# Splitting the mixer's running maximum into three 16-bit parts: on VectorE or on GpSimd

## The chip, the cores and the metric

The kernel runs on one core of a Trainium2 chip. The metric is the device time of one execution in microseconds, as the median of several runs. Everything is one launch; the weights are prepared inside it.

## The reference

Two post-norm decoder layers over `x` of 16 batches x 256 tokens x 256 features, in float32, with a context of the same size:

```python
x = _layernorm(x + _L0_attn_ref(...))    # 16 heads, rotary positions
x = _layernorm(x + _L0_xattn_ref(x, ctx, ctx, ...))    # the mixer
x = _layernorm(x + _L0_ffn_ref(...))     # ternary weights, 8-bit activations
x = _layernorm(x + _L1_attn_ref(...))
x = _layernorm(x + _L1_xattn_ref(x, ctx, ctx, ...))
x = _layernorm(x + _L1_ffn_ref(...))
```

The change is in the second line, the mixer with 8 heads and exponential gates:

```python
csum = jnp.cumsum(jax.nn.log_sigmoid(ftilde), axis=-1)
Dtilde = where(lower triangle, csum[..., :, None] - csum[..., None, :], -inf) + itilde[..., None, :]
max_d = jnp.max(Dtilde, axis=-1, keepdims=True)
D = jnp.exp(Dtilde - max_d)
Ctilde = jnp.einsum('bhid,bhjd->bhij', qh, kh) * D / TAU
maxit = jnp.maximum(jnp.abs(jnp.sum(Ctilde, axis=-1, keepdims=True)), jnp.exp(-max_d))
Htilde = jnp.einsum('bhij,bhjd->bhid', Ctilde, vh) / (maxit + 1e-06)
```

With a = itilde - csum, the exponent is a[j] minus the running maximum of a up to i. So the matrix of decays needs only two rows of 256 numbers for each head.

## The kernel before, in words

A batch of 256 tokens is one unit of work. The 16 batches are dealt to four lanes, and each lane has its own set of tiles (`XO`, `YX`, `PB`, `QK`, `U`, `GN`, `M3` and others; the trace cuts the digit off, so `M3` reads `M`). A lane does its four batches one after the other; they are called rounds 0 to 3 here (`it` in the code). The lanes are interleaved, so that one lane's scores lie beside another's feed-forward layer.

Each batch goes through a list of some 130 steps (`lane_steps`). `PARTS` says which engines have a part in a step. What sets the order is `TURNS`: for every engine a string of digits, each digit a lane, that merges the lanes' lists into one fixed program for that engine. So each engine works through a written order and stops at a wait until it is met, whatever stands behind it. A step in which an engine is named but for which it has no code (for instance `v` of the first attention on VectorE) only takes a digit. `PLACES` gives the PSUM bank of each use.

The steps of the mixer that matter here, for one batch:

- `gates`: TensorE makes the gate inputs (L836). ScalarE makes the log-sigmoid (L1023 to L1029). VectorE, on 8 partitions x 256 elements, runs a sum scan (L1204), an add (L1206), a maximum scan into `G[7]` (L1208) and a subtraction (L1210), whose signal is `max_d`. Then it splits the running maximum into three bfloat16 parts, which go to partitions 0, 32 and 64 of `M3`: copy the high part (L1211), subtract it (L1213), round the rest (L1215), copy that (L1217), subtract it (L1218), copy what is left (L1220, signal `m_lo`).
- `vm`: TensorE centres the values, ScalarE copies them (L1033), GpSimd writes a column of ones (L1354).
- `turn`: TensorE transposes `GT` (L850) after `max_d`; VectorE copies `aT` (L1223); ScalarE makes `eneg` (L1039).
- `decay`, four times: TensorE multiplies a selection matrix with `M3` (L858, L860) and adds the mask (L859, L861); ScalarE takes the exponential (L1047, L1049). The first of the four waits for `m_lo`. Each has L858 twice.
- `mix`: TensorE makes the products of queries and keys (L872); VectorE multiplies them with the decays (L1229).
- `mixv`, `mixnorm`, `mixvar`, `mixscale`: values, transposition, normalization; VectorE's last operation, L1256, is `scaled`.
- `mixout`: GpSimd multiplies by a row and adds the stream (L1357, L1361), which frees the way to the next norm.

GpSimd has besides: `rope` (L1342, the rotary adds), `xb` (L1347, adds a row of biases to the stream of a lane), and the memsets of ones (L1351, L1354).

VectorE's other large work is the maximum of the scores in `max` (L1170, one reduction over 1024 PSUM elements for each pair of heads), for which TensorE makes the scores (L767).

`own` gives an instruction a signal on its engine's own semaphore and `wait_own` waits for it; with it an engine waits for its own earlier result:

```python
n = own(dve.tensor_tensor(Gl[:, 0, :], Gl[:, 7, :], M3[L][0:MH, :], ALU.subtract))
wait_own(n)
n = own(dve.tensor_copy(Mm[L], Gl[:, 0, :]))
wait_own(n)
dve.tensor_copy(M3[L][32:32 + MH, :], Mm[L]).then_inc(mix_dve[L], 1)
```

Of the kernel before, what the change touches and what calls it, by code (L numbers as in the profile page):

```python
# [12 lines left out]
ALU = mybir.AluOpType  # L13
# [11 lines left out]
MH, MHD = 8, 32  # L25
# [20 lines left out]
    "store": "sp", "gates": "pe act dve", "vm": "pe act pool", "turn": "pe dve act", "decay": "pe act",  # L46
# [98 lines left out]
def lane_program(lane):  # L145
# [7 lines left out]
    for at in range(-1, batches):  # L153
# [30 lines left out]
        "0012000311242211332000000000301003011011110110121010221000002010122201022122220311111120331022021233"  # L184
        "3003333122210233221300101321130123213311123333221033203002200300300200023230231203011330110310111113"
        "3131211312221222122122232222333332332320333300033310000003121113002320121221102212211022100200000120"
        "0200110123111133211133333332232313120103022233230000002203310030301111033013101110331110002300122122"
        "1012102221211220021311023333023033120332330031221202230101302112033211221333312311221033220030002000"
        "0002033000123110123203203111111131313111333132112222222220222022020300200203320330033033313303033310"
        "1130000130311111211001222022212220012102211112121112112232323313332333303220300023220000330200310311"  # L190
        "0130313011011303030011331310020122220122021201122221130211303202330112332003322203313013100322132322"
        "1303213331312313021212111030223000030000000023022302330132011113111131113111123212231222012222232000"
        "2220002000220001011113110333301130300003311333132313313300300122022212222021112112111231122333212333"
        "2223333320230000003220003020320033333003333310111011103111100110020122120221202122120232111103311203"
        "1202103213303320333122232101032120110323123320131323311222330220300020030023000032221303130110331011"
        "1111331133111320102122122222222322223333323332133231131333111113011131003000010002001202221220222022"
        "122311113303322333333330032232202310203333330"),
    "dve": (
        "0012210004321344311220000000044111111141223223202220033300330010031010033011020112112002210121201121"
        "3200013100232120100302302123013123321313132112313132010233000223232202223323111333131333130002022012"  # L200
        "0200112111113222332232223300330333120012200001033030001110000011113212213312112111222122030302203333"
        "2202231300331130011330333010120100212010221010321113003211220000321230002010222111332332113121113103"
        "1203030302223032222213232211133310000103330030333312211222112111022220303333222302003011100030320332"
        "1121330111300000011112212231223113211222200022033033222333001300133103033033113201002210022101201113"
        "0002131232102000233021332100202113321123321131111110312330002220330222322302021211001031000331332221"
        "1121231313231130322202022223313330031100000330333301112331020021110001012112121123112332220003332332"
        "2320223022330033130013130033101101200112210101212112020311223030122132300102023213000020213312312311"
        "3113131302203302023223222220331311133133013333001102122111211200200333223023222132213130330033332221"
        "33311222333000"),
    "pool": (  # L210
        "0022211033030032110112210320113332230000110302223111220330012231313102122003331122333010022000111102"
# [1188 lines left out]
```

## Time and profile before

| | |
|---|---|
| median of 3 runs | 1620.26 us |
| lowest and highest | 1614.66 and 1622.32 us |
| the profiled execution | 1622.2 us, its span 1620.4 us |
| mean granted TensorE clock | 0.969 |
| busy: TensorE, VectorE, ScalarE, GpSimd | 1465.2, 1183.2, 950.7, 225.4 us |
| instructions on GpSimd | 233 |

The profile is of one execution. A line such as L858 is a line of the kernel; a helper's line stands for all who call it. A timeline row gives the start and the duration in us, the engine, the line, the operation, what is written and read, how many instructions were merged into the row, and in brackets the idle time before it and who ended that. A granted clock of 1.00 is the full TensorE clock. Spans on GpSimd are rough.

### The profile page before, as it was taken

The numbers are of one execution on the slowest core, as the hardware profiler recorded it, in microseconds if no ns is written. First come the engines' busy times: TensorE is split into PE (matmuls) and PEld (weight loads), VectorE is DVE, ScalarE is ACT, GpSimd is POOL, SyncE is SP. The second block draws the span as 40 slices with busy tenths as digits, with TensorE's granted clock in tenths as the row PEclk, the third lists the DMA queues.
The fourth block names the chain that finished last, engine by engine and source line by source line (L and its number), as shares of the span: only waits on it lengthen the run. The fifth ranks groups of instructions, "written<-read, shape, count | busy, mean of one in ns | idle before, by whom it ended". The sixth has DMA issues, their size and how long they took to land. (4 is left out here: it accounts for less than half of the span.)

```text
span 1620.4 us, 31692 instructions
## 1 busy us (share of the span) xinstructions
PE 1465.2 (90%) x12482; PEld 972.9 (60%) x12482; DVE 1183.2 (73%) x2103; ACT 950.7 (59%) x1701; POOL 225.4 (14%) x233
## 2 busy tenths in 40 slices
PE   7588799899999879899999888998999988898998
PEld 4155556557766556557767555565776656465577
DVE  5978887865568888974765888866565788888632
ACT  3378466674466757566355666656545586655752
POOL 6011100002221011002212210000122111100100
PEclk9699989999999999999999898999999999999999
DMA  8430113322121021521321011331322101133200
GB/s 273 139 102 2 52 47 105 118 60 79 53 69 51 2 63 48 152 67 58 119 73 53 1 47 33 93 108 50 111 72 66 53 2 46 47 97 110 70 1 26
DMA packets 115074, 114.34 MB, mean 71 GB/s; under 512 B 9842, under 2 KB 100722, under 8 KB 114930
## 3 DMA queue, kind: packets, MB, share of 16 engines
q1 hardware_dynamic: 114610, 111.28, 22.4%
q8 instruction: 102, 1.67, 0.4%
q10 hardware_dynamic: 320, 1.05, 0.3%
q14 instruction: 42, 0.34, 0.1%
HBM read 68.91 MB, written 42.99 MB: 69 GB/s over the span
## 5 line engine op out<-in xcount | busy, mean ns | idle before, releaser
L1170 DVE TENSOR_REDUCE nm<-psum 128x4 f16<-128x1024 f32 x384 | 455.1, 1223 | 100.3 <-PE psum L767 99.2
L1005 ACT ACTIVATE PB<-psum 128x1024 f32<-128x1024 f32 x288 | 288.3, 1024 | 87.1 <-PE psum L786 85.7
L804 PE MATMUL psum<-PB,V 128*32 128x256 f32 x2304 | 206.8, 390 | 7.4 <-ACT PB L1005 5.2
L1347 POOL TENSOR_TENSOR XO<-XO,row_b 128x512 f32<-128x512 f32 x80 | 103.2, 1300 | 749.8 <-ACT YX L976 749.8
L767 PE MATMUL psum<-QK 48*128 48x256 f16 x1536 | 140.4, 280 | 46.8 <-DVE nm L1170 22.7
L786 PE MATMUL psum<-QK 49*128 49x256 f16 x1536 | 138.3, 277 | 21.4 <-ACT PB L1005 5.3
L767 PEld LDWEIGHTS psum<-QK 48*128 48x128 f16 x1536 | 58.9, 96 | 109.8 <-DVE nm L1170 38.8
L786 PEld LDWEIGHTS psum<-QK 49*128 49x128 f16 x1536 | 54.2, 95 | 111.4 <-issue 42.1
L930 PE MATMUL psum<-YX,W 128*128 128x256 f32 x512 | 120.0, 385 | 0.0
L804 PEld LDWEIGHTS psum<-PB,V 128*32 128x32 f32 x2304 | 79.9, 110 | 62.6 <-issue 20.0
L938 PE MATMUL psum<-W,PB 128*128 128x256 f32 x512 | 116.3, 382 | 0.0
L1005 ACT ACTIVATE YX<-psum 128x1024 f32<-128x1024 f32 x96 | 98.7, 1028 | 20.3 <-PE psum L786 20.0
L804 PE MATMUL psum<-YX,V 128*32 128x256 f32 x768 | 101.3, 385 | 5.1 <-ACT PB L1005 4.9
L930 PEld LDWEIGHTS psum<-YX,W 128*128 128x128 f32 x512 | 94.4, 190 | 17.3 <-issue 4.2
L938 PEld LDWEIGHTS psum<-W,PB 128*128 128x128 f32 x512 | 95.8, 190 | 13.9 <-issue 1.7
L694 PE MATMUL psum<-W_o,YX 128*128 128x256 f32 x384 | 97.8, 401 | 1.1 <-ACT YX L1012 0.5
L1111 DVE TENSOR_SCALAR XO<-YX,mv,rstd 128x256 f32<-128x256 f32 x192 | 79.5, 457 | 24.6 <-ACT rstd L960 24.3
L1009 ACT ACTIVATE U<-psum 128x512 f32<-128x512 f32 x112 | 66.9, 599 | 50.6 <-PE psum L804 43.3
L681 PE MATMUL psum<-cst,XO 128*128 128x128 f32 x512 | 81.8, 283 | 13.3 <-DMA XO<-in_x 4.2
L694 PEld LDWEIGHTS psum<-W_o,YX 128*128 128x128 f32 x384 | 73.1, 199 | 16.1 <-issue 2.6
L681 PEld LDWEIGHTS psum<-cst,XO 128*128 128x128 f32 x512 | 58.4, 142 | 38.9 <-issue 16.3
L1189 DVE TENSOR_TENSOR YX<-psum,XO 128x512 f32<-128x512 f32 x48 | 33.0, 688 | 64.3 <-PE psum L694 44.4
(171 smaller groups left out, 2675.4 us busy)
## 6 DMA issues: line engine op xcount, KB each, us to landing
QK<-heads_dram SPq DMA_DIRECT2D x96, 512.0 KB, 3.8
heads_dram<-U SPq DMA_DIRECT2D x288, 128.0 KB, 2.0
XO<-in_x SPq DMA_DIRECT2D x16, 256.0 KB, 3.2
YX<-in_ctx SPq DMA_DIRECT2D x16, 256.0 KB, 3.4
out<-XO SPq DMA_DIRECT2D x16, 256.0 KB, 2.5
W<-in_w SPq DMA_DIRECT2D x2, 1024.0 KB, 6.9
heads_dram<-PB ACTq DMA_DIRECT2D x4, 256.0 KB, 9.4
W_gu<-in_w_down SPq DMA_DIRECT2D x1, 1024.0 KB, 5.6
```

The costliest lines, as they stand in the source:

```text
L681: ins = pe.transpose(bank[:, k * TOK + t * P:k * TOK + t * P + P], src[:, t, k * P:(k + 1) * P], ident)
L694: ins = pe.matmul(bank[:, t * DIM:(t + 1) * DIM], xt(k)[:, t * P:(t + 1) * P], w[:, k], start=(k == 0), stop=(k == n - 1))
L767: ins = pe.matmul(b[:, e * 512 + t * TOK:e * 512 + (t + 1) * TOK], QS[L][r, unit, t * P:(t + 1) * P], KS[L][r, unit, :], start=True, stop= ...
L786: ins = pe.matmul(b[:, e * 512 + t * TOK:e * 512 + (t + 1) * TOK], KS[L][r, unit, t * P:(t + 1) * P], QS[L][r, unit, :], start=True, stop= ...
L804: ins = pe.matmul(b[SLOT * j:SLOT * j + SLOT, at:at + TOK], value(L, t, PAIRS * e + u, HEADS, HD, SLOT), src, start=(t == 0), stop=(t == T ...
L930: ins = pe.matmul(b[:, m * TOK:(m + 1) * TOK], W_1[:, k, c:c + P], XT_[L][:, k, :], start=(k == 0), stop=(k == KT - 1))
L938: ins = pe.matmul(b[:, 0:DIM], hid1(L, k)[:, unit * P:(unit + 1) * P], W_2[:, k], start=(k == 0), stop=(k == IT - 1))
L1005: act.activation(weights_of(L, unit), b[:, 0:1024], ACT.Exp, scale=HD ** -0.5)\
L1009: act.activation(flat2(U[L][:, unit - 1:unit + 1, :]), b[:, 0:512], ACT.Copy).then_inc(u_ready[L], 1)
L1111: dve.tensor_scalar(stream(L, it)[:, t], Y[L][:, t], mv[L][:, t, 0:1], rstd[L][:, t:t + 1], ALU.subtract, ALU.mult).then_inc(x_ready[L], 1)
L1170: dve.tensor_reduce(nm[L][:, :, :, unit].rearrange("p t e -> p e t"), b[:, 0:1024].rearrange("p (e t k) -> p e t k", e=2, t=TT), AX.X, ALU ...
L1347: pool.tensor_tensor(stream(L, it), stream(L, it), row_b[:, occ:occ + 1, :].to_broadcast([P, TT, DIM]), ALU.add).then_inc(xb_ready[L], 1)
```

## The change

The six operations go from VectorE's part of `gates` to a new part on GpSimd. They signal on a semaphore of their own, `max_parts`, three times for a batch, and TensorE's first `decay` waits for that. VectorE ends the step with `max_d`. GpSimd's order gets the 16 `gates` steps. The first lines are of the tables, the others of the code; of the digits only GpSimd's are shown.

```diff
-    "store": "sp", "gates": "pe act dve", "vm": "pe act pool", ...
+    "store": "sp", "gates": "pe act dve pool", "vm": "pe act pool", ...
...
     "pool": (
-        "0022211033030032110112210320113332230000110302223111220330012231313102122003331122333010022000111102"
-        "22300113330113322221003203311313022000211111122003232223330001112030023213133332233110122203"),
+        "0002221113330032100011122210320031113332223300010022311112220330233100131102212200033331112223330020"
+        "0011111022223013003330111322221000332331113330222000011111122023222333300001111220002321331133333222"
+        "31012203"),
...
-MIX_DVE = ("a", "max_d", "m_hi", "m_mid", "m_lo", "aT", "c0", "c1", "c2", "c3", "den", "last", "var", "scaled")
+MIX_DVE = ("a", "max_d", "aT", "c0", "c1", "c2", "c3", "den", "last", "var", "scaled")
...
+        max_parts = lane_sem("max_parts")
...
                     if unit == 0:
-                        pe.wait_ge(mix_dve[L], nth(MIX_DVE, it, "m_lo"))
+                        pe.wait_ge(max_parts[L], it * 3 + 3)
...
                     dve.tensor_tensor(GT[L][32:32 + MH, :], Gl[:, 7, :], Gl[:, 6, :], ALU.subtract).then_inc(mix_dve[L], 1)
-                    dve.tensor_copy(M3[L][0:MH, :], Gl[:, 7, :]).then_inc(mix_dve[L], 1)
-                    dve.wait_ge(mix_dve[L], nth(MIX_DVE, it, "m_hi"))
-                    n = own(dve.tensor_tensor(Gl[:, 0, :], Gl[:, 7, :], M3[L][0:MH, :], ALU.subtract))
-                    wait_own(n)
-                    n = own(dve.tensor_copy(Mm[L], Gl[:, 0, :]))
-                    wait_own(n)
-                    dve.tensor_copy(M3[L][32:32 + MH, :], Mm[L]).then_inc(mix_dve[L], 1)
-                    n = own(dve.tensor_tensor(Gl[:, 1, :], Gl[:, 0, :], Mm[L], ALU.subtract))
-                    wait_own(n)
-                    dve.tensor_copy(M3[L][64:64 + MH, :], Gl[:, 1, :]).then_inc(mix_dve[L], 1)
...
+                elif name == "gates":
+                    Gl = G[L]
+                    pool.wait_ge(mix_dve[L], nth(MIX_DVE, it, "max_d"))
+                    pool.tensor_copy(M3[L][0:MH, :], Gl[:, 7, :]).then_inc(max_parts[L], 1)
+                    pool.wait_ge(max_parts[L], it * 3 + 1)
+                    n = own(pool.tensor_tensor(Gl[:, 0, :], Gl[:, 7, :], M3[L][0:MH, :], ALU.subtract))
+                    wait_own(n)
+                    n = own(pool.tensor_copy(Mm[L], Gl[:, 0, :]))
+                    wait_own(n)
+                    pool.tensor_copy(M3[L][32:32 + MH, :], Mm[L]).then_inc(max_parts[L], 1)
+                    n = own(pool.tensor_tensor(Gl[:, 1, :], Gl[:, 0, :], Mm[L], ALU.subtract))
+                    wait_own(n)
+                    pool.tensor_copy(M3[L][64:64 + MH, :], Gl[:, 1, :]).then_inc(max_parts[L], 1)
+                    pool.wait_ge(max_parts[L], it * 3 + 3)
```

The digits of ScalarE, VectorE and SyncE change too. Read out, they move only steps for which that engine has no code. TensorE's digits and `PLACES` are the same. In GpSimd's order, read out the same way, the three `gates` steps that the prediction looks at closest stand as follows (round, step, lane): 1 `mixout` 2, 1 `xb` 0, 1 `v` 0, 1 `xb` 3, **1 `gates` 3**; 3 `mixout` 0, 3 `xb` 1, **3 `gates` 1**; 3 `mixout` 2, 3 `xb` 1, 3 `xb` 3, **3 `gates` 3**.

## Rows read from the trace of the kernel before

**Rows 1.** The page, busy time, share of the span and instructions.

```profile
PE 1465.2 (90%) x12482; PEld 972.9 (60%) x12482; DVE 1183.2 (73%) x2103; ACT 950.7 (59%) x1701; POOL 225.4 (14%) x233
```

**Rows 2.** Waits of TensorE: who waited for whom, total us, times, longest.

```profile
PE psum L767 <- DVE nm L1170: 22.7, 32, 5.1
```

**Rows 3.** Groups by line, VectorE: busy us, mean ns; idle before and its releaser.

```profile
L1213 DVE TENSOR_TENSOR PB<-PB,M 8x256 f32<-8x256 f32 x16 | 6.6, 414 | 0.6
L1218 DVE TENSOR_TENSOR PB<-PB 8x256 f32<-8x256 f32 x16 | 6.6, 413 | 0.5
...
L1220 DVE CAST M<-PB 8x256 bf16<-8x256 f32 x16 | 4.5, 284 | 0.6
L1211 DVE CAST M<-PB 8x256 bf16<-8x256 f32 x16 | 4.5, 281 | 0.5
L1215 DVE CAST PB<-PB 8x256 bf16<-8x256 f32 x16 | 4.5, 280 | 0.5
...
L1217 DVE COPY M<-PB 8x256 bf16<-8x256 bf16 x16 | 3.5, 217 | 0.6
```

**Rows 4.** Timeline, round 0 lane 0, from `max_d` to the first decay.

```profile
99.55 0.41 DVE L1210 TENSOR_TENSOR GN<-PB 8x256 f32<-8x256 f32 x1
...
101.77 0.28 DVE L1220 CAST M<-PB 8x256 bf16<-8x256 f32 x1
...
102.20 0.27 PE L858 MATMUL psum<-M,sel 128*128 128x256 bf16 x1 [0.26 <-DVE M L1220]
```

**Rows 5.** Groups by line, GpSimd, columns as in rows 3.

```profile
L1347 POOL TENSOR_TENSOR XO<-XO,row_b 128x512 f32<-128x512 f32 x80 | 103.2, 1300 | 749.8 <-ACT YX L976 749.8
...
L1342 POOL TENSOR_TENSOR QK<-U 128x256 f32<-128x256 f32 x32 | 36.3, 1158 | 2.5 <-DVE U L1145 2.5
...
L1330 POOL MEMSET GN<- 128x256 f32 x4 | 1.2, 311 | 0.0
```

**Rows 6.** Timeline, round 3 lane 1: `max_d`, the decay, GpSimd's steps.

```profile
1307.87 0.41 DVE L1210 TENSOR_TENSOR GN<-PB 8x256 f32<-8x256 f32 x1
...
1310.52 0.27 PE L858 MATMUL psum<-M,sel 128*128 128x256 bf16 x1
...
1311.17 1.26 POOL L1357 TENSOR_TENSOR XO<-YX,row_b 128x512 f32<-128x512 f32 x1 [45.49 <-DVE YX L1256]
...
1312.57 1.27 POOL L1361 TENSOR_TENSOR YX<-XO 128x512 f32<-128x512 f32 x1
```

**Rows 7.** Timeline, round 1 lane 3: the same, with lane 2's L1256.

```profile
585.54 0.41 DVE L1210 TENSOR_TENSOR GN<-PB 8x256 f32<-8x256 f32 x1
...
594.86 0.40 PE L858 MATMUL psum<-M,sel 128*128 128x256 bf16 x1
...
595.30 0.68 DVE L1256 TENSOR_TENSOR YX<-psum,vr 128x512 f32<-128x512 f32 x1
...
596.06 1.27 POOL L1357 TENSOR_TENSOR XO<-YX,row_b 128x512 f32<-128x512 f32 x1 [38.63 <-DVE YX L1256]
...
598.68 1.31 POOL L1347 TENSOR_TENSOR XO<-XO,row_b 128x512 f32<-128x512 f32 x1
...
600.02 1.26 POOL L1347 TENSOR_TENSOR XO<-XO,row_b 128x512 f32<-128x512 f32 x1
```

**Rows 8.** Timeline, round 3 lane 3 (the last of the 16): the same.

```profile
1373.91 0.41 DVE L1210 TENSOR_TENSOR GN<-PB 8x256 f32<-8x256 f32 x1
...
1377.21 1.27 POOL L1357 TENSOR_TENSOR XO<-YX,row_b 128x512 f32<-128x512 f32 x1 [21.06 <-DVE YX L1256]
1377.24 0.27 PE L858 MATMUL psum<-M,sel 128*128 128x256 bf16 x1 [0.32 <-DVE YX L1256]
```

**Rows 9.** One stretch: busy us and instructions by engine, granted clock, DMA share, GB/s.

```profile
593.00:595.00 2.00, 1.29 (x9) 0.39 (x10) 2.00 (x3) 0.37 (x2) 0.00 (x0) 0.50 0.00 0
```

**Rows 10.** Timeline, round 2 lane 1: `max_d` beside two `xb` steps.

```profile
907.06 3.01 POOL L1347 TENSOR_TENSOR XO<-XO,row_b 128x512 f32<-128x512 f32 x2
...
909.04 1.30 DVE L1210 TENSOR_TENSOR GN<-PB 8x256 f32<-8x256 f32 x1
```

More of the change, by code:

```diff
@@ L45 @@
     "exp": "pe act", "pv": "pe act", "heads": "pe dve", "oT": "pe act", "proj": "pe dve act", "norm": "dve",
-    "store": "sp", "gates": "pe act dve", "vm": "pe act pool", "turn": "pe dve act", "decay": "pe act",
+    "store": "sp", "gates": "pe act dve pool", "vm": "pe act pool", "turn": "pe dve act", "decay": "pe act",
     "mix": "pe dve", "mixv": "pe act", "mixnorm": "pe act dve", "mixvar": "dve act", "mixscale": "dve", "mixout": "pool dve act",
@@ L183 @@
     "act": (
[L184 to L197, printed above, removed]
+        "0012000311242211332000000000300103011011110110112010221000002201012201022122220311111120331022021233"
@@ new lines @@
+        "3003333312221022321300101321130123213311123333322103203000220300300020023230023123011330110310111113"
+        "3131211312222122122122232222333332332320333300003331000000312111302320122121102211222102100200000120"
+        "0200110123111133211133333333222313120103022233230000002200331030301111033301101111033110002300122122"
+        "1012102221221120021131023333023033120333230031221202223010130112033211221333312331122103220030002000"
+        "0002033000123110112320320311111131313111333132112222222222022022020030200203320033033033331303033310"
@@ new lines @@
+        "1113000030311111121000122222212222001102211112121112112232323331332333303222030003220000330020310311"
+        "0113033011011303300011331310020122220122021201122221130211130320233012332003322203313013100322132322"
+        "1303213331331213021212111030223000030000000023022302330132011113111131113111123212223122012222232000"
+        "0222002000022001011113110333301130300003311333132331313300030122022212222201112112111231122333321233"
+        "2223333320223000000320000320320033333003333310111101103111100110020122122021202122210232111110331203"
@@ L198 @@
+        "3120210213303320333122232210103120110323123320131323331122230220300020030023000032221300313111033011"
+        "1111331133111320102122212222222322223333323332133231131133311113011131003000010000201202221220222202"
+        "122311113303322333333330032232220310023333330"),
     "dve": (
-        "0012210004321344311220000000044111111141223223202220033300330010031010033011020112112002210121201121"
-        "3200013100232120100302302123013123321313132112313132010233000223232202223323111333131333130002022012"
@@ L201 @@
-        "0200112111113222332232223300330333120012200001033030001110000011113212213312112111222122030302203333"
-        "2202231300331130011330333010120100212010221010321113003211220000321230002010222111332332113121113103"
+        "0001222110043334411220000000044111111141223223202220033300330010031010033011020112112002210121201121"
+        "3200013100232120100302302123011323321313132112313132010223300023232202223332111333131333130002022012"
+        "0200112111113222332232223300330333120001220001033030001110000011113212213312112111222122030330220333"
@@ L207 @@
[L207 to L208 removed]
+        "1112330111300000011112221231223113211222200022033303222333001300133103033033113201002210022101201113"
+        "0002131232102000233021332100202113321112332131111110312330002220330222322302021211001031000331332221"
+        "1121231313231130322202022223313330003110000330333301112331020021110001012112211123112332220003332332"
```

8 lines of the change are left out of this document (4 added, 4 removed).

## The prediction

> **What bounds the kernel now.** I read the page's busy shares first: TensorE works 1465 us of 1620, VectorE 1183, GpSimd 225 [rows 1]. TensorE leads, but by no wide margin, and 155 us of its idle time are spread in pieces over the span. The table of waits for TensorE shows the kind of piece: one of the commonest is a score matmul that waits for VectorE's maximum, 22.7 us in 32 waits, 0.7 us each [rows 2]. So time taken off VectorE can pay only in such pieces. TensorE takes its steps in a written order, so a step that comes to a wait too early holds everything behind it. The question is therefore not how busy GpSimd is (14%) but how long after `max_d` the three parts are ready, and when TensorE asks for them.
>
> **What is removed.** By line, the six operations take 281, 414, 280, 217, 413 and 284 ns [rows 3], 1.89 us for one batch; with the small gaps the chain runs from 99.96 (end of L1210) to 102.05 (end of L1220) [rows 4], so 2.09 us, 16 times: 33.4 us of VectorE's queue. What VectorE does next starts up to 2.09 us sooner.
>
> **What is added.** Six operations of 8x256 on GpSimd. The trace of before has none of that shape there. The two subtractions: GpSimd's two-input add of 512 elements takes 1.30 us and the rope's of 256 elements, with strided operands, 1.16 us [rows 5]; half of the first, 0.65, and 1.16 are the bounds. I take 0.72, near the first, since these operands are contiguous. The four copies: a 256-element memset takes 0.31 us [rows 5], and half an add is 0.65; I take 0.45, between the two, because a copy reads as well as writes. Four waits on its own semaphore stand inside the chain; the one such pair in the trace (L1357, L1361) leaves 0.14 us between the two operations [rows 6], I take 0.09. The chain is C = 2 x 0.72 + 4 x 0.45 + 4 x 0.09 = 3.6 us, bounds 2.84 (0.65, 0.31, no less than 0.3 of gaps) and 5.5 (1.16, 0.65, 0.6). To that come 0.1 us from VectorE to GpSimd (L1256 ends at 595.98, L1357 starts at 596.06 [rows 7]) and 0.15 us on to TensorE (102.05 to 102.20 [rows 4]): the parts are ready for TensorE at `max_d` + 3.85 us, where it is `max_d` + 2.24 now. GpSimd gets 16 x 3.24 = 52 us more work, which alone costs nothing, as it is idle 86% of the span.
>
> The Trainium skill, GPSIMD Engine Reference, section 4.1 Engine selection, speaks against the change: elementwise work belongs on VectorE, GpSimd being about twice slower for two inputs and roughly at line rate for one. An estimate by that page is 2 x 0.83 + 4 x 0.28 + 0.4 = 3.2 us for the chain, on which the total below would be about 5 us less.
>
> **What TensorE then waits, where GpSimd is free.** For each of the 16 batches I measured S, from the end of L1210 to the first L858 of that batch's first decay step. The first batch has 2.24 us, and there TensorE already waits for L1220 [rows 4]. In order of (round, lane): 2.24, 2.24, 3.11, 3.66; 6.16, 3.83, 4.15, 8.91; 3.47, 2.64, 3.22, 2.71; 7.93, 2.24, 2.68, 2.92. Where the queue is free the new stall is 3.85 - S: 1.61, 1.61, 0.74, 0.19 in round 0; 0.02 in round 1 lane 1; 0.38, 0.63 and 1.14 in round 2 (lanes 0, 2, 3); 1.17 in round 3 lane 2. Sum 7.5 us. Three batches (round 1 lanes 0 and 2, round 3 lane 0) have room.
>
> **What TensorE waits, where GpSimd is not free.** I compared the written orders step by step, leaving out steps for which an engine has no code: those of ScalarE, VectorE and SyncE stay as they are; GpSimd's gets 16 gates steps, each ahead of its batch's memset `vm`. So the costs lie in what stands ahead of a gates step on GpSimd. In 13 cases it is done before `max_d`. In three it is not:
> - Round 1, lane 3. `max_d` is there at 585.95, but ahead stand mixout of lane 2 (L1357 at 596.06, because VectorE's L1256 runs at 595.30), xb of lane 0 (598.68) and xb of lane 3 (600.02 to 601.28) [rows 7]. Without the six operations L1256 comes some 1.7 us sooner, so the gates step starts at 599.7, ends at 603.3, and the decay starts at 603.5, not 594.86: 8.6 us.
> - Round 3, lane 1: `max_d` at 1308.28; VectorE's L1256, now behind the six operations, follows at 1308.5. Then mixout (2.7 us) and xb (1.3), gates from 1313.2 to 1316.8, decay at 1317.0, not 1310.52 [rows 6]: 6.5 us.
> - Round 3, lane 3: `max_d` at 1374.32, L1357 at 1375.1 instead of 1377.21, mixout (2.7 us), two xb (2.5 us), gates 1380.25 to 1383.85, decay at 1384.0, not 1377.24 [rows 8]: 6.8 us.
>
> Sum 21.9 us. While TensorE is stopped that long its clock falls: in the stretch 593 to 595, after the 5.1 us wait that is the longest of [rows 2], the granted clock is 0.50, the lower level of 1.2 GHz, and the decay matmul takes 0.40 us [rows 9, 7] where it takes 0.27 [rows 4]. For two new stalls of that length I add 2.5 us in all. The step ahead of the first of these three is already throttled.
>
> **What else moves.** In round 2, lane 1, the two xb steps of lanes 3 and 2 now run at the same time as VectorE's scan and L1210, and L1210 takes 1.30 us there, not 0.41 [rows 10, 4]. They move behind the gates step, so `max_d` comes 1.8 us sooner and this batch gains 0.6 us. Behind the waiting gates steps stand `vm` (needed by mixv, which waits for the decays anyway), a rope add of lane 3 in round 2 (0.6 us late) and xb steps whose result the projections read tens of us later: nothing for these.
>
> **The sum.** Stalls 7.5 + 21.9, clock 2.5, less 0.6: 31.3 us. Not all arrives at the end. TensorE idles 155 us in 1620 [rows 1], about 0.1 us per us; in the 10 us or so in which the others stay ahead after each of some ten stalls, 1 us is absorbed each: -10. VectorE's lead of 2.09 us pays where TensorE meets a wait for it soon after; at 0.7 us a wait [rows 2], with one such wait in each of the six batches that stall least: -4. Net +17.3. The profiled execution took 1622.2 us outside and 1620.4 in its span, so it would become 1639.5; it lies 2 us above the median of the three runs, 1620.26, so I say 1637.5 for the median.
>
> **The rivals.**
> - Slower still (1646 to 1663, chance 0.17). GpSimd's small operations cost near 5.5 us per chain: the stalls become 26 + 27.6 + 1.3 us, with the clock 57, less 14: +43. For it: a POOL add of 256 elements does take 1.16 us, and operations of VectorE and GpSimd hold each other up, as L1210 shows [rows 10]. Against: most of what VectorE does right after a gates step reads PSUM. The Trainium skill, SBUF — State Buffer, section Who interferes with whom, has the rule that a VectorE instruction with two SBUF inputs and a GpSimd one that reads SBUF exclude each other; by that rule the trace agrees with its 1.30 us, and the six new operations can themselves be held up.
> - No difference (1612 to 1628, chance 0.18). TensorE's stalls are made up from its 155 us of idle time, twice as well as I take it, and the chain costs 2.84 us: 2.5 + 19.6 - 0.6 - 28 = -6, up to +8. Against: with all other engines in written orders, little can run ahead of a stopped TensorE for long.
> - Faster (1595 to 1611, chance 0.08). VectorE's queue is what ends TensorE's waits; each batch returns up to its 2.09 us, at one to two waits of 0.7 us per batch some 14 us: 1606. It decides only if the parts are not late: the chain at or below 2 us, and GpSimd's queue free in the three late batches. What stands ahead in those three makes that unlikely.
> - The change doing less than it says (the order around it kept, so no stall of the three): the written order for GpSimd in the diff rules it out, so it has no share of its own.
>
> **How the numbers follow.** The forecast (queue blocked three times, small stalls elsewhere, +9 to +26) has 0.57. About 0.5%, 8 us, is what a measurement of this kernel tells from no change. Slower by over that: 0.57 + 0.17 = 0.74; within: 0.18; faster: 0.08. The range takes the forecast's own, 1629 to 1646, down to most of no difference (1617) and up into the slower rival as far as 1656.
>
> **What would show it.** TensorE's waits for GpSimd's M, none now, sum to about 30 us with three of 6 to 9 us near 594, 1311 and 1378; GpSimd's busy time is 277 us, a subtraction there 0.72 us, a copy 0.45; VectorE's busy time falls by 30 us; L1210 in round 2 lane 1 takes 0.41. It is wrong if the first decay of those three batches doesn't wait for M, or if TensorE's idle time is no larger than 155 us in spite of the stalls.

## The result and the profile after

The changed kernel takes 1647.49 us (four runs, 1644.72 to 1651.77), the kernel before 1619.37 with its fourth run: ratio 1.0173, interval 1.0151 to 1.0195, so 28 us slower. The profiled execution took 1644.72 us, its span 1642.9, the mean granted clock 0.960 (before: 1622.2, 1620.4 and 0.969). It is the fastest of the four, so what the profile shows is rather less than the loss by the medians.

The page of the changed kernel, busy time and instructions, answers to [rows 1]:

```profile
PE 1469.3 (89%) x12482; PEld 975.6 (59%) x12482; DVE 1150.9 (70%) x2007; ACT 950.5 (58%) x1701; POOL 271.7 (17%) x329
```

VectorE has 32.3 us less, 2 more than its six operations took (16 x 1.89), so on the whole nothing else of VectorE's got slower beside GpSimd's new work. GpSimd has 46.3 us more, and TensorE the same work in a longer span. GpSimd's order has one move besides the 16 `gates` steps: in rounds 0 to 2 lane 0's memset `vm` comes later, behind that lane's `gates`. TensorE waits for GpSimd's M and for nothing else of GpSimd's, so this move costs nothing that shows. The lines after the change are two higher in TensorE's part (L858 is now L860) and up to L1210 (now L1212); on GpSimd L1347 (`xb`) is now L1353, L1357 and L1361 (`mixout`) are L1363 and L1367.

GpSimd's groups of 8x256 by line (busy us, mean ns, idle before) answer to [rows 3] and to what [rows 5] had to bound:

```profile
L1340 POOL TENSOR_TENSOR PB<-PB,M 8x256 f32<-8x256 f32 x16 | 10.6, 659 | 1.3
L1345 POOL TENSOR_TENSOR PB<-PB 8x256 f32<-8x256 f32 x16 | 10.5, 659 | 1.2
L1344 POOL COPY M<-PB 8x256 bf16<-8x256 bf16 x16 | 6.5, 404 | 1.0
L1347 POOL CAST M<-PB 8x256 bf16<-8x256 f32 x16 | 6.2, 389 | 1.0
L1338 POOL CAST M<-PB 8x256 bf16<-8x256 f32 x16 | 6.2, 386 | 63.9 <-DVE GN L1212 63.9
L1342 POOL CAST PB<-PB 8x256 bf16<-8x256 f32 x16 | 6.2, 386 | 1.0
```

A subtraction takes 0.66 us, a copy 0.39 to 0.40. From the start of L1338 to the end of L1347 it is 3.22 or 3.23 us in 14 of 16 batches, and 3.39 at most.

TensorE's waits (total, times, longest) have a new row:

```profile
PE psum L860 <- POOL M L1347: 28.1, 10, 9.7
```

The timeline of the changed kernel, at the places of [rows 4, 7, 10, 6, 8]:

```profile
103.38 0.29 PE L852 MATMUL psum<-cst,GN 40*128 40x40 f32 x2 [1.64 <-DVE GN L1212]
103.60 1.37 PE L806 MATMUL psum<-PB,V 128*32 128x256 f32 x16
...
106.67 0.37 PE L860 MATMUL psum<-M,sel 128*128 128x256 bf16 x1 [0.73 <-POOL M L1347]
...
584.39 0.42 DVE L1212 TENSOR_TENSOR GN<-PB 8x256 f32<-8x256 f32 x1
...
593.22 1.26 POOL L1363 TENSOR_TENSOR XO<-YX,row_b 128x512 f32<-128x512 f32 x1 [33.85 <-DVE YX L1248]
...
595.83 1.31 POOL L1353 TENSOR_TENSOR XO<-XO,row_b 128x512 f32<-128x512 f32 x1
...
597.16 1.26 POOL L1353 TENSOR_TENSOR XO<-XO,row_b 128x512 f32<-128x512 f32 x1
...
598.37 0.39 POOL L1338 CAST M<-PB 8x256 bf16<-8x256 f32 x1
...
601.20 0.39 POOL L1347 CAST M<-PB 8x256 bf16<-8x256 f32 x1
...
601.73 0.37 PE L860 MATMUL psum<-M,sel 128*128 128x256 bf16 x1 [9.65 <-POOL M L1347]
...
916.21 0.41 DVE L1212 TENSOR_TENSOR GN<-PB 8x256 f32<-8x256 f32 x1
...
1320.43 0.37 PE L860 MATMUL psum<-M,sel 128*128 128x256 bf16 x1 [6.03 <-POOL M L1347]
...
1398.67 0.37 PE L860 MATMUL psum<-M,sel 128*128 128x256 bf16 x1 [6.62 <-POOL M L1347]
```

In round 1 lane 3, `max_d` is there at 584.8 and the first copy starts at 598.37, after steps of other batches (the first of them waits for VectorE) and the lane's own `xb`. TensorE stands 9.65 us. The other two blocked batches cost 6.03 and 6.62. Together 22.3 of the 28.1 us are in three batches of 16. The first decay after each is at 0.37 us where [rows 4] has 0.27; in round 1 lane 3 it was slow before too, 0.40 [rows 7].

That is the second thing to see: stretches of 3 us in the changed kernel (columns as in rows 9; the granted clock is the third number from the end):

```profile
104.00:107.00 3.00, 2.27 (x26) 0.86 (x16) 1.45 (x2) 0.67 (x2) 2.38 (x6) 0.54 0.57 122
107.00:110.00 3.00, 3.00 (x22) 2.43 (x21) 0.92 (x1) 2.07 (x7) 0.00 (x0) 0.50 0.31 17
110.00:113.00 3.00, 3.00 (x22) 2.28 (x18) 0.96 (x1) 1.77 (x6) 0.00 (x0) 0.50 0.85 319
...
1318.00:1321.00 3.00, 0.57 (x5) 0.54 (x6) 0.00 (x0) 0.00 (x0) 2.14 (x6) 0.50 0.00 0
1321.00:1324.00 3.00, 3.00 (x22) 2.43 (x19) 0.00 (x0) 2.31 (x8) 0.00 (x0) 0.50 0.01 3
```

From about 104 to 118 us TensorE works at 1.2 GHz, 13.7 us. In the trace of before the clock stays at 1.00 there. The fall comes ahead of the wait of 0.73 us for M, which lasts from 105.94 to 106.67: the row of 104 to 107 is already at 0.54, and the 16 matmuls of L806 that start at 103.60 take 1.37 us, where the same 16 take 1.07 in the kernel before (from 100.33). What lies ahead of the fall is the 1.64 us in which TensorE idles for `max_d`, and the kernel before has that too (1.69 us). So the wait for M did not bring the fall on; whether it made the stretch longer is taken up with e12_late_once.

Over the whole span, (1 - mean clock) x 2 x span is the time at the lower level: 100 us before, 131 us after in the profiled executions. Every execution has its span and mean clock on record, so the same can be had for all of them; it is in a column of the table of the experiments. Within the kernel before, over 89 executions in four series, the time goes with it: from 77 to 131 us at the lower level, 1610 to 1634 us, by a straight line 0.33 us of run time for each us at the lower level (correlation 0.87).

VectorE's order is the same in both kernels, so the same instruction can be looked up in each timeline. The table gives how much later than in the kernel before it starts (us); the two columns on the right are experiments told below.

| VectorE's instruction | starts, before | after | e1_order | e4_warm |
|---|---|---|---|---|
| first scan, round 0 lane 0 | 96.9 | +3.3 | +0.9 | -0.6 |
| proj, round 0 lane 1 | 113.0 | +9.5 | +7.4 | +0.5 |
| mixscale, round 1 lane 2 | 595.3 | -2.9 | -1.0 | -9.4 |
| first up, round 1 lane 2 | 609.5 | +6.5 | -0.9 | -1.5 |
| mixscale, round 3 lane 0 | 1310.4 | +2.1 | +0.1 | -7.0 |
| proj, round 3 lane 2 | 1321.6 | +13.9 | +3.0 | +0.6 |
| mixscale, round 3 lane 2 | 1376.4 | +13.1 | +0.6 | -1.6 |
| quant, round 3 lane 2 | 1383.7 | +23.1 | +2.9 | +5.8 |
| last proj | 1580.3 | +22.5 | +2.9 | +5.7 |

Four steps of the staircase, 6.2, 9.3, 11.8 and 10.0 us, add up to more than the whole. Between them the changed kernel also wins time: from round 0's lane 2 to 300 us it comes back from +10.4 to +1.4, where the kernel before has a stretch at the lower clock (204 to 216) and the changed one has none. After the last mixer nothing is made up any more: +22.6 at 1412 is +22.5 at 1580. The way back by 300 us isn't the stalls being made up: e3_order_hi_only, told below, has no stall and comes back as far, from +4.2 at 151 us to -5.8 at 300, and this one from +10.1 to +1.4. The 3.3 us ahead of the first scan are not of the change, as no changed instruction has run by then; in e1_order they are 0.9 and in e4_warm -0.6.

### The profile page after: what moved, and what is told of

The parts are those of the page before. It is cut to its first block and busy times, and to the rows that moved or that the text cites. A ratio compares the mean times of both kernels' runs of the same rounds, so it can differ in the third digit from the quotient of the medians.

```text
span 1642.9 us, 31707 instructions
## 1 busy us (share of the span) xinstructions
PE 1469.3 (89%) x12482; PEld 975.6 (59%) x12482; DVE 1150.9 (70%) x2007; ACT 950.5 (58%) x1701; POOL 271.7 (17%) x329
## 3 DMA queue, kind: packets, MB, share of 16 engines
q8 instruction: 102, 1.67, 0.4%
## 5 line engine op out<-in xcount | busy, mean ns | idle before, releaser
L1353 POOL TENSOR_TENSOR XO<-XO,row_b 128x512 f32<-128x512 f32 x80 | 102.5, 1292 | 727.8 <-ACT YX L978 727.7
L806 PE MATMUL psum<-PB,V 128*32 128x256 f32 x2304 | 208.5, 392 | 7.9 <-ACT PB L1007 5.0
L788 PE MATMUL psum<-QK 49*128 49x256 f16 x1536 | 139.9, 279 | 21.9 <-ACT PB L1007 5.2
L806 PEld LDWEIGHTS psum<-PB,V 128*32 128x32 f32 x2304 | 80.1, 110 | 63.2 <-issue 20.3
L806 PE MATMUL psum<-YX,V 128*32 128x256 f32 x768 | 103.4, 391 | 5.7 <-ACT PB L1007 5.4
L932 PEld LDWEIGHTS psum<-YX,W 128*128 128x128 f32 x512 | 94.4, 190 | 17.3 <-issue 4.2
L940 PEld LDWEIGHTS psum<-W,PB 128*128 128x128 f32 x512 | 95.8, 190 | 13.9 <-issue 1.7
L696 PE MATMUL psum<-W_o,YX 128*128 128x256 f32 x384 | 94.1, 389 | 1.5 <-ACT YX L1014 1.1
```

The lines of the kernel that those rows point to most:

```text
L696: ins = pe.matmul(bank[:, t * DIM:(t + 1) * DIM], xt(k)[:, t * P:(t + 1) * P], w[:, k], start=(k == 0), stop=(k == n - 1))
L788: ins = pe.matmul(b[:, e * 512 + t * TOK:e * 512 + (t + 1) * TOK], KS[L][r, unit, t * P:(t + 1) * P], QS[L][r, unit, :], start=True, stop= ...
L806: ins = pe.matmul(b[SLOT * j:SLOT * j + SLOT, at:at + TOK], value(L, t, PAIRS * e + u, HEADS, HD, SLOT), src, start=(t == 0), stop=(t == T ...
L932: ins = pe.matmul(b[:, m * TOK:(m + 1) * TOK], W_1[:, k, c:c + P], XT_[L][:, k, :], start=(k == 0), stop=(k == KT - 1))
L940: ins = pe.matmul(b[:, 0:DIM], hid1(L, k)[:, unit * P:(unit + 1) * P], W_2[:, k], start=(k == 0), stop=(k == IT - 1))
L1353: pool.tensor_tensor(stream(L, it), stream(L, it), row_b[:, occ:occ + 1, :].to_broadcast([P, TT, DIM]), ALU.add).then_inc(xb_ready[L], 1)
```

## The experiments

Twelve kernels, all timed in five rounds against the kernel before, whose median was 1621.54 us in the series of e1 to e4, 1620.02 in that of e5 to e8, 1619.33 in that of e9 to e11 and 1620.01 in that of e12.

| kernel | median us | ratio to before | interval | mean clock | at lower level, us |
|---|---|---|---|---|---|
| e1_order | 1630.01 | 1.0054 | 1.0034 to 1.0075 | 0.966 | 123 |
| e2_hi_only | 1623.71 | 1.0015 | 0.9998 to 1.0031 | 0.966 | 110 |
| e3_order_hi_only | 1605.62 | 0.9904 | 0.9882 to 0.9925 | 0.974 | 84 |
| e4_warm | 1630.19 | 1.0053 | 1.0035 to 1.0071 | 0.975 | 83 |
| e5_order_warm | 1619.43 | 0.9990 | 0.9972 to 1.0009 | 0.972 | 95 |
| e6_before_warm | 1615.75 | 0.9973 | 0.9955 to 0.9991 | 0.974 | 81 |
| e7_shadow | 1648.65 | 1.0157 | 1.0129 to 1.0184 | 0.957 | 137 |
| e8_scan_bf16 | 1612.86 | 0.9943 | 0.9921 to 0.9965 | 0.973 | 91 |
| e9_scan_hold | 1607.67 | 0.9932 | 0.9909 to 0.9954 | 0.976 | 89 |
| e10_scan_hold_warm | 1604.24 | 0.9906 | 0.9878 to 0.9935 | 0.976 | 79 |
| e11_shadow_late | 1628.76 | 1.0062 | 1.0040 to 1.0084 | 0.969 | 103 |
| e12_late_once | 1626.27 | 1.0032 | 1.0009 to 1.0055 | 0.965 | 108 |

The mean clock is that of the profiled execution. The last column is the time at the lower clock level as the mean over all executions of the kernel; in the same way it is 137 us for the changed kernel and 101, 99, 99 and 99 for the kernel before in its four series. The changed kernel was timed in a series of its own (before: 1619.37), so a difference of medians to it is good to some 4 us.

### The order of GpSimd's steps

e1_order changes only the digits of GpSimd. Read out, in three places:

```diff
-1 mixout 2, 1 xb 0, 1 v 0, 1 xb 3, 1 gates 3
+1 xb 3, 1 gates 3, 1 mixout 2, 1 xb 0, 1 v 0
-3 mixout 0, 3 xb 1, 3 gates 1
+3 xb 1, 3 gates 1, 3 mixout 0
-3 mixout 2, 3 xb 1, 3 xb 3, 3 gates 3
+3 xb 3, 3 gates 3, 3 mixout 2, 3 xb 1
```

> The changed kernel with GpSimd's written order mended in three places: in round 1 lane 3, round 3 lane 1 and round 3 lane 3 the lane's own xb and gates steps stand ahead of the other lane's mixout. Nothing else differs. Theory (the queue ahead of those three gates steps makes most of the loss): TensorE's three long waits for M (9.65, 6.03, 6.62 us) fall below 1.5 us each, and the kernel takes 1620 to 1629 us, some 22 us less than the changed one. Rival (the loss is the 3.2 us chain itself, in all 16 batches, and long waits are absorbed anyway): no more than 8 us less, 1640 or above.

1630.0 us, 17.5 less than the changed kernel (19 by the ratios 1.0173 and 1.0054). TensorE's waits in e1_order:

```profile
PE psum L860 <- POOL M L1347: 11.1, 10, 2.0
```

The waits fell by 17.0 us and the longest is 2.0. The time is 1 us above the range given and on the theory's side: three places in a written order made 17.5 of the 28 us. The steps at 595, 1310 and 1376 in the table shrink from 9.3, 11.8 and 10.0 to 0.1, 2.9 and 2.3. The one at 97 to 113 stays (6.5).

### Without the chain

e2_hi_only leaves out the middle and low parts (in this and the next kernel only the high part is used for the decays):

```diff
                     pool.tensor_copy(M3[L][0:MH, :], Gl[:, 7, :]).then_inc(max_parts[L], 1)
-                    pool.wait_ge(max_parts[L], it * 3 + 1)
-                    ...
-                    pool.wait_ge(max_parts[L], it * 3 + 3)
+                    pool.wait_ge(max_parts[L], it + 1)
```

> The changed kernel in its own order, but GpSimd does only the first of the six operations (the high part); the middle and low parts of the maximum are left out and their rows of M3 stay zero. The chain is 0.4 us instead of 3.2. Theory: the three blocked batches still wait, each 2.8 us less, and the small stalls of the other batches go: 1625 to 1635. Rival (the chain is all that costs): as fast as before or faster, 1620 or below.

1623.7 us, 1.3 below the theory's range and not at the rival's (1620 or below); it is still no faster than before. Its waits for M are 13.8 us in 3 (the longest 6.8): with a chain of 0.39 us the three blocked batches go on waiting, and no other batch waits at all. So the queue alone takes up what relieving VectorE gives.

e3_order_hi_only is e2 with the order of e1.

> Both: the mended order of e1_order and only the high part on GpSimd (middle and low parts left out). What is left of the change is that VectorE has 2.09 us less to do in each of 16 batches. Theory (VectorE's relief pays in TensorE's waits for it, about 0.5 to 0.9 us a batch): 1605 to 1614. Rival (relief of VectorE is worth nothing): 1617 to 1622.

1605.6 us, 16 less than before and inside the range. Relief of VectorE, with the order as mended, is worth a half of the 33 us that it takes off, once nothing waits for GpSimd. I had allowed 4 us for it. A part of the 16 is the order's, as e8_scan_bf16 and e9_scan_hold show below.

### TensorE's clock

e4_warm keeps the order and the waits of the changed kernel:

```diff
                     if unit == 0:
+                        for _ in range({(1, 3): 28, (3, 1): 24, (3, 3): 24, (0, 0): 4, (0, 1): 6, (0, 3): 3, (2, 1): 4, (2, 3): 2}.get((it, L), 0)):
+                            pe.matmul(b[:, 0:512], identb[:, :], sel[:, 0:4, :].rearrange("p h q -> p (h q)"), start=True, stop=True)
                         pe.wait_ge(max_parts[L], it * 3 + 3)
```

> The changed kernel in its own order, with TensorE kept at work while it waits for M: before the wait, 2 to 6 matmuls of 512 columns in five batches of rounds 0 and 2 and 24 to 28 in the three blocked batches, written into the bank that the decay then overwrites. The waits stay as long. Theory (a part of the loss is TensorE at its lower clock after each stop, 131 us at the lower level instead of 101): the stretches at 0.50 behind those batches go, and the kernel takes 5 to 12 us less, 1635 to 1642. Rival (the clock is not part of it): 1645 to 1650.

1630.2 us: 17.3 less, more than the theory's 5 to 12. Round 3 lane 1 in e4_warm, first the timeline (two lines higher, L862 for L860), then two stretches:

```profile
1302.63 0.41 DVE L1214 TENSOR_TENSOR GN<-PB 8x256 f32<-8x256 f32 x1
...
1311.26 0.28 PE L862 MATMUL psum<-M,sel 128*128 128x256 bf16 x1 [0.68 <-POOL M L1349]
```

```profile
1311.00:1314.00 3.00, 2.74 (x34) 2.30 (x34) 0.52 (x1) 1.98 (x7) 0.33 (x2) 1.00 0.03 8
1314.00:1317.00 3.00, 3.00 (x41) 2.25 (x40) 2.96 (x8) 2.97 (x10) 0.00 (x0) 1.00 0.00 0
```

`max_d` to the decay is 8.2 us in this timeline, as without the matmuls (8.28 in the changed kernel), but the clock stays at 1.00 and the decay takes 0.28. In the table its steps are 1.1, 7.8, 7.7 and 7.4 where the changed kernel has 6.2, 9.3, 11.8 and 10.0: the difference, 5.1 + 1.5 + 4.1 + 2.6 = 13.3 us, is the clock's part at these four places in these two profiles. Time at the lower level falls from 131 to 81 us; that is 0.35 us of run time for each of these. Over all executions it falls from 137 to 83.

e5_order_warm has both edits, the matmuls only in the five batches with small stalls.

> The mended order of e1_order (1630.0 us) and TensorE kept at work, 2 to 6 matmuls of 512 columns, before the wait for M in five batches of rounds 0 and 2 (lanes 0, 1, 3 and lanes 1, 3). Theory (what is left of the loss is the 3.2 us chain plus a low-clock stretch that the 1.3 us idle after round 0 lane 0 brings on, 13.7 us long in e1_order): the stretch at 102 to 118 us goes and the kernel takes 4 to 8 us less than e1_order, 1622 to 1626. Rival (the clock costs something only after the long stops): 1628 to 1632.

1619.4 us, 10.6 less than e1, 2.6 below the theory's range, and the same as before (ratio 0.9990, its interval takes in 1). With the two edits four kernels make a square: neither 1647.5, order 1630.0, warm 1630.2, both 1619.4 (ratios 1.0173, 1.0054, 1.0053, 0.9990).

e6_before_warm is the control, the same matmuls ahead of `turn`'s wait for `max_d` in the kernel before:

```diff
+                    for _ in range({(0, 0): 6, (0, 3): 6, (2, 1): 10, (3, 2): 10}.get((it, L), 0)):
+                        pe.matmul(b[:, 0:512], identb[:, :], sel[:, 0:4, :].rearrange("p h q -> p (h q)"), start=True, stop=True)
                     pe.wait_ge(mix_dve[L], nth(MIX_DVE, it, "max_d"))
```

> Control: the kernel before with the same kind of matmuls where its own TensorE idles ahead of the turn step, 6 each in round 0 lanes 0 and 3, 10 each in round 2 lane 1 and round 3 lane 2 (idle 1.7 to 2.5 us there). Theory (keeping TensorE at work pays only where a stop would lower the clock; of these four places round 0 lane 3 and round 2 lane 1 have such a stretch, 10.2 us each): 1614 to 1619, 3 to 7 us less than before. Rival (the gain of e4_warm was particular to the changed kernel): 1620 to 1624.

1615.8 us, ratio 0.9973: inside the theory's range. The trick pays 4 us in the kernel before too, at other places than in e4 and e5, so a part of their gain need not be of the change; how large a part, no run shows.

e12_late_once puts one delay into the kernel before:

```diff
+                    for k in range(4 if (it, L) == (0, 0) else 0):
+                        wait_own(own(dve.tensor_copy(Gl[:, 3 + k % 2, :], Gl[:, 1, :])))
                     dve.tensor_copy(M3[L][64:64 + MH, :], Gl[:, 1, :]).then_inc(mix_dve[L], 1)
```

> The kernel before with one delay in one place: in round 0 lane 0, VectorE makes four extra copies of 8x256 (about 1.3 us) ahead of the last part, so that the first decay of the whole run comes 1.3 us late, as in the changed kernel, where TensorE has idled 1.7 us three us earlier. The other 15 batches stay. Theory (such a delay lets the granted clock fall to 0.50 for a stretch, 13.6 us in the changed kernel, and costs far more than itself): the stretch from some 104 us on is at 0.50 and the heads step of lane 1, at 107.4 us before, and all behind it shift by 4 to 6 us; the median is 1622 to 1627. Rival (the delay costs itself at most): no such stretch, shift 1.3 us, median 1619 to 1622.

1626.3 us, 6.3 above before, interval 1.5 to 8.9 us, inside the theory's range. From its trace, TensorE's matmuls behind the 1.67 us in which it idles for `max_d`, VectorE's four copies, and a stretch:

```profile
105.23 1.93 PE L804 MATMUL psum<-PB,V 128*32 128x256 f32 x16
...
106.57 1.23 DVE L1221 COPY PB<-PB 8x256 f32<-8x256 f32 x4
```

```profile
107.00:110.00 3.00, 2.87 (x25) 1.98 (x22) 2.86 (x7) 1.25 (x4) 0.00 (x0) 0.50 0.46 60
```

There is a stretch at 0.50, but the delay didn't make it. The 16 matmuls of L804 from 105.23 take 1.93 us instead of 1.07, so the clock is already low more than a us ahead of the copies, and it is back by 112. The copies cost no wait either: with TensorE at half its clock, the first decay waits 0.14 us, where it waits 0.26 in [rows 4]. The heads step of lane 1 shifts by 2.8 us against the scan ahead of it, not 4 to 6. So the mechanism that I wrote down, a late part that lowers the clock, isn't shown. Over all executions the kernel has 9 us more at the lower level than the kernel before, some 3 us of time at 0.33 each; with 1.3 us for the delay itself that makes 4 of the 6.3, and the rest is open.

All the profiles together say more of this place, behind the first `max_d`:

| TensorE at the first decay | kernels | stretch at 0.50, us |
|---|---|---|
| waits 0.7 to 1.4 us for the parts | changed kernel, e1_order, e7_shadow | 13.7, 13.7, 13.7 |
| matmuls put ahead of that wait | e4_warm, e5_order_warm | none, 3.4 |
| waits no longer than before | before, e2, e3, e8, e9, e11 | none, 3.4, 3.4, none, none, 10.2 |
| the same, with matmuls ahead of `turn` | e6_before_warm, e10_scan_hold_warm | none, none |
| the delay of e12_late_once | e12_late_once | 6.8 |

The idle 1.6 to 1.7 us for `max_d` stand in all but the fourth row. So the fall comes or doesn't come behind that idle time, with or without a late part. The longest stretches go with a wait in them, but e11_shadow_late, told below, has 10.2 us of it with no such wait (0.26 us), and shifts by 4.4 us there where the changed kernel shifts by 6.2:

```profile
104.00:106.00 2.00, 2.00 (x16) 1.60 (x15) 1.77 (x2) 1.30 (x5) 1.76 (x4) 0.50 0.35 35
```

That a wait for the parts makes the stretch longer is likely from these single profiles, not shown.

### GpSimd's work and VectorE's side by side

e7_shadow leaves VectorE its six operations and gives GpSimd six of the same shapes on a scratch tile:

```diff
+                elif name == "gates":
+                    pool.wait_ge(mix_dve[L], nth(MIX_DVE, it, "max_d"))
+                    m7, g0, g1 = (scratch[0:MH, n] for n in range(3))
+                    hi, mid = scratch_b[0:MH, 0], scratch_b[0:MH, 1]
+                    wait_own(own(pool.tensor_copy(hi, m7)))
+                    wait_own(own(pool.tensor_tensor(g0, m7, hi, ALU.subtract)))
+                    ...
```

> The kernel before with GpSimd's order of the changed kernel and six operations of the same shapes on GpSimd, after max_d, on a scratch tile that nobody reads; VectorE keeps its own six and TensorE waits for them. So GpSimd has the added work and order, and no one waits for its result. Theory (GpSimd's added work by itself costs nothing): 1618 to 1624. Rival (contention between GpSimd's and VectorE's operations is a part of the loss): 1627 or more.

1648.7 us: the rival's case, and as slow as the changed kernel, although nobody waits for GpSimd. VectorE's groups in e7_shadow, mean ns of one, against [rows 3]:

```profile
L1222 DVE CAST M<-PB 8x256 bf16<-8x256 f32 x16 | 9.2, 578 | 0.5
L1220 DVE TENSOR_TENSOR PB<-PB 8x256 f32<-8x256 f32 x16 | 9.2, 577 | 0.5
L1217 DVE CAST PB<-PB 8x256 bf16<-8x256 f32 x16 | 9.2, 576 | 0.5
L1215 DVE TENSOR_TENSOR PB<-PB,M 8x256 f32<-8x256 f32 x16 | 7.7, 482 | 0.6
...
L1213 DVE CAST M<-PB 8x256 bf16<-8x256 f32 x16 | 4.5, 281 | 0.5
```

The casts of 0.28 take 0.58 where a GpSimd operation runs beside them, the subtractions 0.48 and 0.58 for 0.41, and only L1213, which starts first, keeps its time. GpSimd loses too: the first cast takes 485 ns for 386 in the changed kernel, the subtractions 719 and 708 for 659. The chain on VectorE is 2.82 us for 1.89, the parts come 0.9 us late, and time at the lower clock goes to 142 us. It was not the clean control I meant. Nor is it what happens in the changed kernel, where VectorE has no chain for GpSimd's to meet and its busy time fell by all that was taken off.

e11_shadow_late moves GpSimd's six behind VectorE's:

```diff
-                    pool.wait_ge(mix_dve[L], nth(MIX_DVE, it, "max_d"))
+                    pool.wait_ge(mix_dve[L], nth(MIX_DVE, it, "aT"))
```

> e7_shadow (1648.7) with one difference: GpSimd's six operations on the scratch tile start after aT, which VectorE makes behind its own six, not after max_d. The added work and GpSimd's order stay, the overlap with VectorE's six goes. Theory (what cost 28 us in e7 was that the two chains ran at the same time and held each other up, 2.8 us instead of 1.9 on VectorE, and the low clock that this brought on): VectorE's casts there take 0.28 us again, the decays wait no longer, 1618 to 1630. Rival (GpSimd's added work or order itself costs): 1640 or more.

1628.8 us, inside the range: 20 of e7's 28 us were the collision and what it brought on. VectorE's six have the times of [rows 3] again. What is left is 9 us over before. 4.4 us of shift come at the stretch at 0.50 behind the first `max_d`, shown above. Besides, there are two long waits among TensorE's:

```profile
PE psum L739 <- POOL QK L1345: 3.7, 1, 3.7
PE psum L886 <- POOL V L1367: 2.9, 1, 2.9
```

These are a rope add and a `vm` memset that stand behind a gates step. So added work in a written queue isn't free even if its result is not used: it delays what is behind it. In the changed kernel the gates step starts earlier and neither wait is long, so this is a cost of e11's own.

### A version that beats both

Any value m may stand for the running maximum as long as the decays and exp(-m) use the same one: it cancels in the quotient but for the 1e-6. So it need not be split, only rounded once, and the maximum scan can write the rounded value itself. e8_scan_bf16 has neither the six operations nor anything on GpSimd:

```diff
-                    n = own(dve.tensor_tensor_scan(Gl[:, 7, :], GT[L][0:MH, :], GT[L][0:MH, :], NEG, ALU.max, ALU.max))
+                    n = own(dve.tensor_tensor_scan(M3[L][0:MH, :], GT[L][0:MH, :], GT[L][0:MH, :], NEG, ALU.max, ALU.max))
                     wait_own(n)
-                    dve.tensor_tensor(GT[L][32:32 + MH, :], Gl[:, 7, :], Gl[:, 6, :], ALU.subtract).then_inc(mix_dve[L], 1)
-                    ...
+                    dve.tensor_tensor(GT[L][32:32 + MH, :], M3[L][0:MH, :], Gl[:, 6, :], ALU.subtract).then_inc(mix_dve[L], 1)
```

> A version in which the split isn't needed: the maximum scan writes its result as bfloat16 straight into M3's first part, and the subtraction for exp(-max_d) reads the same rounded value. Any m may be taken for the maximum so long as the decays and exp(-max_d) use the same one, since it cancels in the quotient but for the 1e-6. Middle and low parts are left out, GpSimd does nothing, TensorE waits for max_d. It has VectorE's whole relief, as e3_order_hi_only (1605.6), and no chain behind max_d. Theory: 1602 to 1607. Rival (part of e3's gain came from the moved xb and gates steps): 1608 to 1614.

1612.9 us: 7 less than before, but 6 above the theory's range. It is the rival's case (1608 to 1614): part of e3's gain came from the moved steps. e9_scan_hold adds the order of e1 and a bare wait on GpSimd:

```diff
+                elif name == "gates":
+                    pool.wait_ge(mix_dve[L], nth(MIX_DVE, it, "max_d"))
```

> e8_scan_bf16 (1612.9) with GpSimd's mended order of e1_order and, in its gates step, only the wait for max_d, so that in round 2 lane 1 the two xb steps of lanes 3 and 2 no longer run beside VectorE's scan and two-input operations (1.64, 1.31 and 1.30 us in e8's trace instead of 0.68, 0.41 and 0.41). Middle and low parts are left out as in e8. Theory (the difference between e8 and e3_order_hi_only, 1605.6, is that collision and the low clock behind it): L1210 there takes 0.41 us and the kernel 1603 to 1608. Rival (the difference lies elsewhere): 1611 to 1614.

1607.7 us, within the theory's range. Its VectorE timeline in round 2 lane 1, the scan and the subtraction that follows:

```profile
899.00 0.68 DVE L1209 TENSOR_TENSOR_SCAN M<-GN 8x256 bf16<-8x256 f32 x1
899.72 0.41 DVE L1211 TENSOR_TENSOR GN<-M,PB 8x256 f32<-8x256 bf16 x1
```

The same two in e8_scan_bf16:

```profile
900.74 1.64 DVE L1208 TENSOR_TENSOR_SCAN M<-GN 8x256 bf16<-8x256 f32 x1
902.42 1.30 DVE L1210 TENSOR_TENSOR GN<-M,PB 8x256 f32<-8x256 bf16 x1
```

Holding back two `xb` steps frees the scan and the subtraction of 1.9 us. The ratios of e8 and e9 to before (0.9943 and 0.9932) are from different series and their intervals overlap, so the medians' 5 us are not sure. e10_scan_hold_warm puts 6 matmuls ahead of four `turn` waits.

> e9_scan_hold with 6 matmuls of 512 columns ahead of TensorE's wait for max_d in round 0 lanes 0 and 3, round 2 lane 1, round 3 lane 2. Middle and low parts left out as in e8. Theory (stretches at the lower clock begin at such waits and cost the rest): 2 to 6 us less than e9. Rival (no low-clock stretch begins there any more): within 2 us of e9.

1604.2 us, 3.4 less than e9 in the same series, as the theory had it, though here too the intervals overlap. The time at the lower level is 77 us in both profiles, but e9's is of its second fastest execution of ten; over all executions it is 89 us for e9 and 79 for e10, and 10 us at 0.33 each is the difference. Against before the ratio is 0.9906, interval 0.9878 to 0.9935: 15 us. It is the fastest that keeps the mixer's sum whole; e3 at 1605.6 rounds only one of the two uses of m.

## Why the prediction was right, and where it was off

The sign, the order of size and the range (1617 to 1656) held; 1647.5 is 10 us above the forecast of 1637.5, and 1.5 above what the range gave to the forecast's own case (1629 to 1646). The main mechanism, three `gates` steps held up in GpSimd's order, is right and was tested. That the total is no further off is in part luck, as errors of 8 to 11 us stand on both sides. By its steps:

- **The chain.** C was put at 3.6 us from 0.72, 0.45 and 0.09; it is 3.22 from 0.66, 0.39 and 0.07. The parts are ready 3.43 us after `max_d`, not 3.85. The Trainium skill, GPSIMD Engine Reference, section 4.1 Engine selection, led to 3.2, and the trace agrees with that sum; of its two ratios, about twice for two inputs and about the same for one, neither fits alone: at this size a subtraction costs 1.6 times VectorE's (659 for 413 ns), a cast 1.4 times (386 for 281) and the copy between 16-bit tiles 1.9 times (404 for 217).
- **Small stalls.** 7.5 us forecast, 5.8 measured (28.1 less the three blocked ones).
- **The blocked queue.** 8.6, 6.5 and 6.8 us forecast, 9.65, 6.03 and 6.62 measured: 21.9 against 22.3. The sum is closer than its terms (1.1 too few, 0.5 too many, 0.2 too many). Reading the order of the steps against the times of before gave each to about a us, and e1_order shows that it is the cause of 17.5 us.
- **Round 2 lane 1.** L1212 takes 0.41 us for 1.30 as said. The gain did not come whole, since TensorE still waits 1.97 us there.
- **The clock.** Here a term of the sum was far too small. "For two new stalls of that length I add 2.5 us in all" counts only the long stops, and too little for them. By the four places, e4_warm against the changed kernel, the clock is 13 us; by 31 us more at the lower level at 0.35 us each, 11 us; by 38 us more over all executions at 0.33 each, 13 us. I take 11 to 13, so 8 to 11 too few. The stretch at round 0 lane 0, 5 of the 13, wasn't in the sum at all. It comes behind an idle time that the kernel before has too, so how much of it is the change's isn't shown.
- **Absorption, -10.** None is to be seen. The shift behind the last mixer stays to a tenth of a us, and what the changed kernel wins back by 300 us a kernel without stalls wins as well. The step that said so, 1 us for each stall from TensorE's idle share, took an average over the span for what is on offer at that place.
- **VectorE's lead, -4.** Worth 16 us by e3 (with the order mended and no chain); 7 to 12 by e8 and e9. With -12 in the place of -4 and nothing absorbed, the sum is 5.8 + 22.3 + 11 - 12 = 27, and 28 was measured. But -12 was picked from 7 to 16 with the result known, so this is no test: with 7 and 16 the sum is 32 and 23. The absorption that didn't come took the forecast 10 us too low, the small term for VectorE's relief about 8 too high; these cancel for the most part, and the clock's 8 to 11 is what is left.
- **The rivals.** The slower one named the right time and the wrong cause: the chain was shorter than forecast, not near 5.5 us, and no GpSimd operation of the chain was held up (its 3.22 us hardly vary), nor VectorE by them (its busy time fell by 32.3 us for 30.2 taken off). "No difference" fails with the missing absorption. "Faster" named the points from which it decides, a chain at or below 2 us and a free queue; e3 meets both, and is faster.

Open: which stretches at the lower clock come in a given execution. Some come and go with no cause at hand, as at 682 to 700 us, 17 us long in the profiles of e1_order and e4_warm and 3 in that of before. The first scan, which no changed instruction precedes, starts 0.8 us earlier to 4.8 us later than in the kernel before, by profile. So terms of 2 us can't be told from single profiles.

## What to carry to other kernels

Where every engine works through a written order, ask of moved work what stands ahead of it in the new queue, and when that is released; the free share of the engine (86% here) says nothing. Compare the new latency with the slack at the consumer, one instance at a time, and count the ones without slack. Before a chain is moved off a busy engine, ask whether it is needed: a rounded value used in both places made it superfluous and won 7 us by itself, 12 with the order mended and 15 with filler matmuls, where moving it lost 28.

## What the hardware showed that I had not expected

- Idle pieces of TensorE of 1.6 us, far below the 9.65 us of the longest stop, were followed by 10.2 us (e11_shadow_late) and 13.7 us (changed kernel) at 0.50, with the shift growing by 4.4 and 6.2 us; in other kernels with the same idle piece the clock stayed at 1.00. Filling such waits with matmuls that nobody reads took 17 us off the changed kernel and 4 off the kernel before. The Trainium skill, TensorE: Matmul & The Clock Gate, section What's actually happening, has it that the gate goes by how busy the array has lately been; the traces agree, 137 us at the lower level without and 83 with them.
- Operations of VectorE and GpSimd on eight partitions hold each other up: 281 ns become 577 for a cast, 0.68 us becomes 1.64 for a scan beside an `xb` step, and two chains of six run at the same time cost as much (28 us) as moving one; 20 of these go when the second chain starts later.
- GpSimd's small operations were steady: 3.22 us from first to last in 14 of 16 batches.
